# One half of the softmaxed shares is turned a tile later in the last layers; a batch's rows are read earlier; a new order of the work

## The reference

```python
x = L0_attn_hidden
x = _layernorm(x + _L0_attn_ref(x, ...))
x = _layernorm(x + _L0_ffn_ref(x, ...))
x = _layernorm(x + _L1_attn_ref(x, ...))
x = _layernorm(x + _L1_ffn_ref(x, ...))
```

```python
h = shift_token(x)
q, k, v = split_heads(h @ wqkv)          # 8 heads of 64
q, k = rotary_xpos(l2norm(q) * qs, l2norm(k) * ksc)
sim = einsum('bhwid,bhwjd->bhwij', bq, bk)   # windows of 64 queries, 128 keys
attn = softmax(where(mask, -max, sim))
x = x + (attn @ bv) @ wo
h = layernorm(shift_token(x)) @ w1 + b1
a, g = split(h, 2)
x = x + (a * gelu(g)) @ w2 + b2
```

## Time and profile before

| | us |
|---|---|
| median of 3 runs | 1913.15 |
| lowest and highest of them | 1906.26, 1914.19 |
| the profiled execution, its own time | 1924.5 |
| its span, first to last instruction | 1922.5 |
| PE busy, share of the span | 1614.5, 84% |
| ACT busy | 1190.7, 62% |
| DVE busy | 1114.0, 58% |
| POOL busy | 790.1, 41% |
| mean granted TensorE clock, share of full speed | 0.900 |

### The profile page before, as it was taken

How to read it: one execution, slowest core, us unless ns; L and a number is a source line. 1 busy time by engine, 2 the same in 40 slices (tenths; PEclk the granted TensorE clock), 3 DMA queues, 4 the chain that set the end, 5 groups by cost and what they waited for, 6 DMA issues and landing times.

```text
span 1922.5 us, 37968 instructions
## 1 busy us (share of the span) xinstructions
PE 1614.5 (84%) x13911; PEld 1054.3 (55%) x13911; DVE 1114.0 (58%) x2041; ACT 1190.7 (62%) x2786; POOL 790.1 (41%) x656
## 2 busy tenths in 40 slices
PE   3789767856987999999888998999778997797986
PEld 2222326735565765734665775544556876455563
DVE  5611655154776546666787456755776546575663
ACT  2598754611665898487645886688546872365571
POOL 1563233032544556166226355376116431452540
PEclk8699888965989999899898999899899997689897
DMA  5100004600113441011012540010003540110100
GB/s 163 64 2 1 1 28 128 180 27 13 38 41 115 126 125 41 7 42 26 18 36 85 158 129 24 17 28 24 12 29 104 161 120 10 38 34 19 37 19 12
DMA packets 77466, 109.58 MB, mean 57 GB/s; under 512 B 13935, under 2 KB 38755, under 8 KB 77155
## 3 DMA queue, kind: packets, MB, share of 16 engines
q1 hardware_dynamic: 71587, 98.24, 18.1%
q0 software_dynamic: 4096, 8.40, 1.5%
q10 hardware_dynamic: 1600, 0.52, 0.1%
HBM read 74.40 MB, written 15.93 MB: 47 GB/s over the span
## 4 chain that ended last, share of the span: by engine, by line
PE 49%; DVE 18%; ACT 10%; POOL 9%; issue 8%; SPq 2%; DMA 2%; DVEq 0%; POOLq 0%; ACTq 0%
PE PX L1383 6%; PE PX L968 5%; PE PX L1404 5%; PE PX L1201 3%; PE PX L1214 3%; POOL middle_arena L2489 3%; PE PX L1019 3%; PE PX L1305 2%; PE PX L1328 2%; ACT front_arena L1537 2%; PE PX L1443 2%; PE PX L1317 2%; PE PX L1422 2%; PE PX L1433 2%; POOL front_arena L2457 2%
## 5 line engine op out<-in xcount | busy, mean ns | idle before, releaser
L1537 ACT ACTIVATE front_arena<-PX 128x1024 f32<-128x1024 f32 (+3 forms) x288 | 225.9, 823 | 70.4 <-PE PX L1019 68.5
L2457 POOL TENSOR_TENSOR front_arena<-front_arena,tri 128x256 f32<-128x256 f32 x192 | 155.3, 820 | 206.9 <-ACT front_arena L1537 206.3
L2519 POOL TENSOR_TENSOR back_arena<-back_arena 128x512 f32<-128x512 f32 x96 | 144.9, 1514 | 203.6 <-DVE back_arena L2298 203.1
L1713 ACT ACTIVATE back_arena<-PX,fnm 128x128 f32<-128x128 f32 x384 | 136.0, 375 | 57.9 <-DVE fnm L2306 57.7
L1383 PE MATMUL PX<-wqkv,hT 128*128 128x512 f32 x288 | 161.7, 654 | 7.2 <-ACT hT L1672 6.2
L968 PE MATMUL PX<-front_arena 128*32 128x512 f32 (+3 forms) x1152 | 134.1, 540 | 20.4 <-POOL front_arena L2457 17.7
L2524 POOL TENSOR_TENSOR fy<-fm,minus_half 128x16 f32<-128x16 f32 x48 | 141.2, 2943 | 20.2 <-DVE fm L2324 18.8
L2306 DVE TENSOR_REDUCE fnm<-PX 128x4 f32<-128x512 f32 x96 | 66.3, 690 | 127.0 <-PE PX L1404 125.5
L1404 PE MATMUL PX<-back_arena 64*64 64x128 f32 x1536 | 108.5, 282 | 0.6 <-ACT back_arena L1756 0.6
L1404 PEld LDWEIGHTS PX<-back_arena 64*64 64x64 f32 x1536 | 84.7, 136 | 39.6 <-issue 39.1
L2489 POOL DMA_INDIRECT middle_arena<-y_rows,rows x64 | 64.5, 1007 | 97.9 <-DMA y_rows<-middle_arena 80.1
(11 more groups left out here) (443 smaller groups left out, 4071.4 us busy)
## 6 DMA issues: line engine op xcount, KB each, us to landing
W<-in_W SPq DMA_DIRECT2D x48, 258.0 KB, 3.5
W<-in_W SPq DMA_DIRECT2D x48, 256.0 KB, 3.2
back_arena<-back_arena SPq DMA_DIRECT2D x96, 128.0 KB, 2.4
middle_arena<-in_W SPq DMA_DIRECT2D x44, 258.0 KB, 3.2
middle_arena<-in_W SPq DMA_DIRECT2D x44, 256.0 KB, 2.9
xpos<-x_tables SPq DMA_DIRECT2D x48, 128.0 KB, 2.0
y_rows<-middle_arena SPq DMA_DIRECT2D x20, 256.0 KB, 3.8
middle_arena<-x_rows SPq DMA_DIRECT2D x8, 512.0 KB, 4.5
```

The costliest lines, as they stand in the source:

```text
L1537: act.activation(pb[:, :, 0:n], p[:, :, 0:n], ACT.Exp, scale=INV_SQRT_HD).then_inc(freed(b, "S", half, g, kc, jp), 1)
L1713: ins = act.activation(y.fP[:, h, :], p[:, c:c + 128], ACT.Exp, bias=y.fnm[:, h:h + 1], accum_out=y.fden[:, h:h + 1])
L2457: pool.tensor_tensor(pb, pb, tri[:, :].unsqueeze(1).to_broadcast([128, 2, 128]), ALU.mult).then_inc(of_front(b, "masked"), 1)
L2519: pool.tensor_tensor(y.T1[k % 2][:, hs, :], y.T1[k % 2][:, hs, :], y.T2[:, hs, :], ALU.add).then_inc(of_back(b, "rot"), 1)
```

## The change

Three things are changed.

First, `p,1`, the turning of the second four heads' shares of a tile, leaves the end of a round. It is now in the next tile's round, behind `q`, so between the scores of half 0 and those of half 1. For the last tile of a layer it stands alone in round 10. On ACT, the copy of these shares moves from ahead of the exponentials of half 0 to behind them. SP's transfers of a tile's shifted values and of the next tables, which were given out at `p,1`, are now given out at `p,0`. The name under which a bank is booked for `p,1` goes back one tile more.

Second, SP starts reading batch 1's rows (16 transfers) right behind the first weights. Before, they stood behind the zeroing of `x_rows` and the second set of weights.

Third, `RUNS` and `BANKS` are new tables. Beside what the first two items need, they move whole labels. Batch 1's norm, transposes and projection stand ahead of the end of batch 0's norms instead of behind them. Batch 2's front begins beside the end of batch 0's expert part, ahead of batch 0's last layers. The 16 scatters of batch 0 stand together behind the eighth triangle product of batch 1 beside them (before, 8 scatters stood ahead of the eighth). Batch 3's last layers start ahead of the rest of batch 2's.

```diff
--- before.py
+++ after.py
@@ -231,6 +231,8 @@
                 add(("s", l, i, 0), 1.5, 1.5, 0.6, 0.7)
             if fresh:
                 add(("q", l, i), 1.1, 1.2, 2.3, 1.2)
+            if out_:
+                add(("p", l, i, 1), 1.2, 1.5, 0.6)
             if scores:
                 add(("s", l, i, 1), 1.5, 1.5, 0.6, 2)
             if fresh:
@@ -250,7 +252,6 @@
                 add(("v", l, i), 1.1, 1.2, 0.6)
             if scores:
                 add(("p", l, i, 0), 1.2, 1.2, 0.6)
-                add(("p", l, i, 1), 1.2, 1.5, 0.6)
             if i == 7:
                 add(("hF", l, 0), 1.2, 1.5, 1.2)
             if i == 9:
@@ -295,41 +296,41 @@
 
 
 RUNS = """
-F13 G2 F2 G1 F2 G2 F3 B1 F3 G1 F2 G1 F2 G1 F2 G2 F6 G1 F6 G1 F5 G1 F1 G1
...
+F3 G1 F5 G1 F3 G1 F4 G2 F3 B1 F4 G2 F2 G2 F4 G1 F7 G1 F2 G1 F4 G1 F3 G2
...
@@ -375,22 +376,22 @@
 
 
 BANKS = """
-4026026026026025640260260260426026026502602602460260260260526026020642060260260260260260246026052602602
...
+4026026026026206250462062062506206206420620620652062602602604265026026260262062062062062064205620620620
...
@@ -419,7 +420,7 @@
             else:
                 back = {"s": 2, "p": 2, "o": 3, "t": 1}
                 if n in back:
-                    rest = (rest[0], rest[1] - back[n], *rest[2:])
+                    rest = (rest[0], rest[1] - back[n] - (n == "p" and rest[2]), *rest[2:])
                 t.add("S", b, "f" + n, *rest)
     assert len(t.at) == len(BANKS), len(t.at)
     return t
@@ -830,13 +831,12 @@
                             load_x(b, range(2))
                             for dst, s in first[HALF_FIRST:]:
                                 sp.dma_start(dst, s).then_inc(sg("weights1"), 16)
+                            load_x(1)
                             sp.wait_ge(sg("zeros"), ZEROS)
                             sp.dma_start(x_rows.rearrange("(p t) d -> p t d", t=SLOTS),
                                          main.Nb[:, 0:1, :].to_broadcast([128, SLOTS, 128])).then_inc(sg("x_zero"), 16)
                             for dst, s in second:
                                 sp.dma_start(dst, s).then_inc(sg("weights2"), 16)
-                            yield front_at(b, "toT", 0)
-                            load_x(1)
                             yield front_at(b, "x1", 0)
                             load_x(2)
 
@@ -893,7 +893,7 @@
                         for l in range(DEPTH):
                             for t in range(NT):
                                 k = (PLACE[b] * DEPTH + l) * NT + t
-                                yield back_at(b, "p", l, t, 1) if t >= 2 else back_at(b, "v", l, t)
+                                yield back_at(b, "p", l, t, 0) if t >= 2 else back_at(b, "v", l, t)
                                 if k + TRING < len(of) * DEPTH * NT:
                                     is_free(sp, b, "fq", l, t)
                                     is_free(sp, b, "fk", l, t)
@@ -1453,6 +1453,9 @@
                             if fresh:
                                 yield back_at(b, "qk"[r], l, i)
                                 project_step(b, l, i, "qk"[r])
+                            if out_ and r == 0:
+                                yield back_at(b, "p", l, i, 1)
+                                turn_scores(b, l, i - 3, 1)
                         if out_:
                             yield back_at(b, "o", l, i)
                             value_step(b, l, i - 3)
@@ -1464,9 +1467,8 @@
                             yield back_at(b, "v", l, i)
                             project_step(b, l, i, "v")
                         if scores:
-                            for r in range(2):
-                                yield back_at(b, "p", l, i, r)
-                                turn_scores(b, l, i - 2, r)
+                            yield back_at(b, "p", l, i, 0)
+                            turn_scores(b, l, i - 2, 0)
 
                 def chain(*parts):
                     for p in parts:
@@ -1770,12 +1772,12 @@
 
                     for i in range(NT + 3):
                         scores, fresh, out_, turn = 0 <= i - 2 < NT, i < NT, 0 <= i - 3 < NT, 0 <= i - 1 < NT
-                        if out_ and scores:
-                            yield back_at(b, "s", l, i, 0)
+                        if scores:
+                            yield back_at(b, *(("q", l, i) if fresh else ("s", l, i, 0)))
+                            exps(b, l, i - 2, 0)
+                        if out_:
+                            yield back_at(b, *(("s", l, i, 1) if scores else ("p", l, i, 1)))
                             turned_scores(b, l, i - 3, 1)
-                        if scores:
-                            yield back_at(b, *(("q", l, i) if fresh else ("s", l, i, 1)))
-                            exps(b, l, i - 2, 0)
                         if fresh:
                             yield back_at(b, *(("s", l, i, 1) if scores else ("k", l, i)))
                             square(b, l, i, 0)
@@ -1797,10 +1799,8 @@
                             yield back_at(b, *(("p", l, i, 0) if scores else ("v", l, i)))
                             values_in(b, l, i)
                         if scores:
-                            yield back_at(b, "p", l, i, 1)
+                            yield back_at(b, "p", l, i, 0)
                             turned_scores(b, l, i - 2, 0)
-                            if i == NT + 1:
-                                turned_scores(b, l, i - 2, 1)
 
                 def last_layers(of):
                     for b in of:
```

100 lines of the change are left out of this document (50 added, 50 removed).

## The result

The changed kernel took 1925.25 us (median of 5 runs, 1922.75 to 1929.61) beside 1913.15 of the kernel before (5 runs as well): a ratio of 1.006, with a 95% interval of 1.0032 to 1.0087. Measured again on another chip it was 1.0044 (1.0024 to 1.0064). The forecast was 1897 with a range of 1876 to 1920, so it missed on the wrong side: 8 to 12 us slower where 16 faster were forecast.

What follows compares the result with a forecast made beforehand. PE was taken as the likely bound, but a ring of engines in batch 3's lone rounds. Terms -17 + 3 - 4 - 2 + 0 - 2 + 6 = -16 took the median 1913.15 to 1897 us, range 1876 to 1920.

Steps and rivals of the forecast that it cites:

- Batch 3's last layers start earlier: Ahead of batch 3's last layers PE has 20 us less of batch 2's work, so they start earlier: -17 us.
- The tail: Batch 3's last layers: returning work +5, four more table loads +5, better clock -7, together +3 us.
- The clock credit of 7 in the tail: Batch 3's last layers: fuller PE gets clock 0.90 instead of 0.86, 10 us less, of which 7 counted.
- The new wait: Value products in mixed rounds wait for ACT's copy, now behind the exponentials; about 16 late rounds: +6 us.
- Other waits for the turning: PE's 30.6 us of waits at the turning mostly give no time back: -2 us, bounds -8 and 0.
- the ring: DVE, POOL, PE and ACT in turn set the 10.29 us of batch 3's lone rounds; removing PE's wait shortens none.
- The start: Batch 1's early rows let its first work fill holes of DVE and PE: -2 us.
- Batch 2's front beside batch 0's experts: 7.0 us of batch 2's front work fits into 19.5 us of PE waits around batch 0's experts: -4 us.
- The second: Rival, chance 0.13: value products late by 0.7 us on average over 48 rounds, +34, giving 1925 us.
- The first: Rival, chance 0.22: work moved into batch 3's last layers costs in full there, +18 instead of +3, giving 1912 us.
- The third and the fifth: Rivals, together 0.15: all gains add, 1880 us; or moving the turning gives back all 30.6 us, below 1880.
- the fourth: Rival, chance 0.05: each of four table loads costs 1.4 us more in ring-bound rounds, +6, giving 1903 us.

Runs made afterwards that it cites:

- middle_new: Kernel before with the new order only from batch 2's expert part (985 us) to batch 3's second front norm (1350 us), turning unmoved, 7 banks changed: 1.0066.
- tail_new: Kernel before with the new order only from the start of batch 3's experts (1419 us) on, turning unmoved, 8 banks changed: 0.9968.
- head_new: Kernel before with batch 1's rows read early and the new order up to about 192 us, turning unmoved, 2 banks changed: 1.0004.
- move_undone_b: Changed kernel's order with the turning of half 1 back at the round's end, 22 banks chosen anew: 1.0192 of the kernel before.

## Why the prediction was wrong, point by point

- **Batch 3's last layers start earlier, -17 (-20 to -8): the step that failed most.** With the new end alone it was -4.0 against before's second profile and -7.2 against its first, outside its bounds in both. The moved products were priced one by one against a full PE. But batch 2's rounds took their place in the linear attention's stretch (151 more products there in the changed kernel), where PE works at a lower clock (0.78) and waits for batch 3's chain. In the changed kernel PE's wait ahead of that first product fell from the 7.19 us of the earlier trace rows to 3.40.
- **The middle had no term.** The first description of the change named what moved at the start, at batch 0's experts and at the end, and the sum took the stretch between 985 and 1350 us as unchanged. The new run table moves 114 products out of batch 2's experts there and 202 into the stretch behind them. `middle_new` prices this at +12.7 us, about half of the 24 to 28 us between the forecast of -16 and the measured 8 to 12; the term above, short by 10 to 13, is most of the other half. A sum over named moves is no sum over a new table.
- **The tail, +3 (-2 to +10): right on average.** +2.0 in the pair and +2.1 in the table; single pairs reach from -5.7 to +9.1. The tail has 8 table loads instead of 4, as forecast. A round can close in 10.30 us and take up hidden products and two table loads. Not each one does: three rounds of `tail_new` between 1678 and 1713 us take 11.63, 11.36 and 10.78, where before's second profile has 10.30. By the Trainium skill (ScalarE: Activation LUTs, What ACT_TABLE_LOAD costs) a switch of tables has a drain of about 1.4 us beside its load. A round with two switches still closed in 10.30 us, so there neither the load nor such a drain showed in the time; in the rows ACT's next instruction starts 0.01 us behind each of the two loads. The 5.1 us for four loads were probably too much; no run has them alone.
- **The clock credit of 7 in the tail** was taken against a profile whose tail had 0.86. Before's second profile has 0.90 there, and the two others with the old end 0.90 and 0.93. Part of this gain was noise of the profile of before, and the step from the profile's own time to the median (11.35 us as if spread evenly) hid it.
- **The new wait, +6 (0 to +16): right in place and in size.** 12.5 us at the value product in the first profile of the changed kernel, in 13 places against 16 counted. The size is in part luck: 16 rounds at the 2.0 us of the round read would have been 32, not the 16 given as all of them, and the places turned out at 1.0 us each. Its share of the end time isn't known: the one edit that removes most of it costs more.
- **Other waits for the turning, -2: the row's 30.6 us went to 6.0**, nearly all, and the rounds of batch 3 didn't get shorter. So the reading of the ring was right. What the term is worth in the time no run has alone.
- **The start, -2 (-4 to +2): within its bounds.** Some 8 us were won by 190 us and given back later:

```profile
27.03 1.09 PE L936 MATMUL PX<-ident,back_arena 128*128 128x128 f32 x4 [5.03 <-DVE back_arena L1861]
...
38.34 3.39 PE L1127 MATMUL PX<-ident,front_arena 128*128 128x128 f16 x32 [9.37 <-DVE front_arena L1966]
```

  Batch 1's turning stands in PE's hole (15.01 us in the earlier trace rows, now 9.37 and a product in it), 17 us earlier than before. `head_new` measures it alone: 1.0004, so 1 us with an interval of 4 to either side.
- **Batch 0's scatters, 0: nothing speaks against it.** The wait of 12.32 us went and came back as 11.34 us ahead of batch 1's turning at 301.07, which before waited 1.24. No run has this part alone.
- **Batch 2's front beside batch 0's experts, -4 (-7 to 0).** The hole of the earlier trace rows of 12.24 us became 14.06, the one of 7.24 is filled, and batch 0's last layers started 2.1 us earlier. No run has this part alone.
- **The rivals.** The second had the sign and, by accident, the time (1925), but not the cause: it wanted 34 us at the value product, and 12.5 came. The first (moved work costs in full in the tail, +18) is refuted by the table: +2.1 on average, +9.1 at most; the tail was a part that worked. The third and the fifth (all gains add) fail with the -17, and the fourth (a switch of tables costs more) with the round of 10.30 us that holds two.

The parts measured alone give -6 + 12.7 + 1 = +8 us, beside the measured 8 to 12, with an uncertainty of the sum of some 8 us. That this agrees is no proof that they add up: all three were measured with the turning unmoved, and the whole new order with the turning unmoved (`move_undone_b`) is 37 us slower than before. So either the parts that no run has alone (192 to 985 us and 1350 to 1419 us) cost the other 29 without the move, or the parts depend on each other, or its banks do it. What the moved turning is worth in its own order stays open, and so does how much of the 12.7 us the middle costs beside the moved turning; the old middle in the changed kernel would have told, and wasn't run.

## What to carry to other kernels

When a hand-made order is replaced as a whole, lay both orders over the same milestones and price every stretch between them; a stretch without a term can decide the sign, as it did here. Here work taken out of stretches in which PE also waits gave little back there (125 products, 4 to 7 us), what stayed ran at a lower clock, and products put behind the experts lengthened that stretch by 28 to 32 us. Profile the kernel before twice, and look at the granted clock of each timed run, before a few per mille are priced. And a place in such an order, its bank table and its run table are one fitted thing: one part changed alone cost 24 to 59 us, in either direction, and says little of what the part is worth.

## What the runs showed of the hardware that was not expected

- Two executions of one program differed by 20.2 us in span (1922.5 and 1902.3). PE was busy 24.8 us longer in the slower one, at a mean granted clock of 0.900 instead of 0.913, and idle 4.6 us less. 12.1 us of it lay in two stretches in which PE is busy 85 to 88%; batch 3's experts, where it is busy 98% at a clock of 1.00, agreed to 0.2 us.
- With 42 or 125 of 1540 products taken out of a stretch of 227 to 230 us, its granted clock was 0.85 to 0.87 in four profiles, beside 0.90 to 0.93 in four with all of them.
- Another assignment of PSUM banks, with the order of all instructions the same, cost 1.9%. In its profile PE is idle 1940.0 - 1610.3 = 329.7 us, beside 308.0 and 312.6 in the two of before. That PE waits there for banks whose readers run late is likely, but its waits weren't added up by bank.
